# Interleaving the last norm of a transformer tower over three tiles on the Vector engine, and filling TensorE with constant products through a recurrence

## The chip, the cores and the metric

The kernel runs on one core of a Trainium2 chip. A core has TensorE (PE: matrix products; its weight loads are shown apart as PEld), the Vector engine (DVE), the Scalar engine (ACT), GpSimd (POOL) and SyncE (SP, which issues DMAs). The engines run side by side and wait for each other on semaphores; each takes its own instructions in their order in the program. The metric is the device time of one execution in microseconds (us); the median over the runs is quoted.

## The reference: what is computed

A small vision tower over 32 images of 3x64x64 pixels. Sixteen patches of an image and a class token make 17 tokens of 192 features, 544 tokens in all. Four parts follow, each with a layer norm in front and the input added back:

1. attention with mixing of the heads' scores before and after the softmax;
2. a mixture of 16 experts (top 4 of a softmax router);
3. a recurrence over the 17 tokens of every image;
4. a mixture of 8 experts (the best one for each token).

The change touches parts 3 and 4:

```
def step(h, ins):                      # part 3, for token t = 0..16
    bv, dc, ij = ins
    h_next = dc * quat_rotate(h, bv) + ij
    return (h_next, h_next)
_, hs = scan(step, h0, (biv_t, dec_t, inj_t))
y = (hs - mean(hs)) / sqrt(var(hs) + 1e-05) * gamma + beta
h = h + y
x = layernorm(h)                       # part 4
logits = x @ router_w                  # 8 experts; argmax picks one
out = combine over experts of relu(x @ Wi_e) @ Wo_e
h = h + out
```

So between the recurrence and the router there are two norms over the 192 features of each token: that of the states `hs` (norm 3 in the code) and that of the sum `h` (norm 4).

## The kernel before, in words

The 544 tokens lie in five tiles: four of 119 rows (seven images) and one of 68. Activations are kept both with a token in a partition (for norms) and turned, with a feature in a partition (for products). A product in single precision is made of rounded high and low parts, so a turned tile is taken out of PSUM twice: ACT writes the high part (`high_turned`, L428), DVE subtracts it from the original for the low part (`low_turned`, two instructions, L959 and L961).

All engines' programs are written out by hand, in the order in which the lines are called; nothing reorders them. Around the change they are as follows.

- **Walls.** PE multiplies the normed input by the weights of the recurrence (`wall`, through L1651) into PSUM banks 0 to 7. ACT and DVE take the results out and make, for every token, a 3x3 rotation with its decay, `rmat`. PE has nothing to do meanwhile.
- **Scan.** DVE alone computes the states, 16 steps in two chains of eight images: a product (L1430) and a sum (L1435) for each chain. From step 9 on PE runs `hold`: products of constants (L1927, 128x128 by 128x272) whose result nobody reads, 4 a step and 2 in the last, released by the step's product.
- **Norms.** PE turns the states back to a token in a partition (`states_turned(i)`, L2024, L2026, and L2028 with L2034 for tile 2, which lies over both halves of the partitions), one PSUM bank a tile. For each tile DVE then does, under `states_normed`, `summed` and `shifted`: statistics (bn_stats, L943), their mean and variance (bn_aggr, L944), `xw = (state - mean) * gamma` (L1444), reciprocal of the deviation (L1451), `h = xw * rstd + h` (L1454), bn_stats and bn_aggr again for norm 4, the reciprocal (L1461) and the shift `xn_off` (L1463). With the two of `low_turned` these are eleven. ACT supplies the square roots (`root(3, i)` and `root(4, i)`, L423), the normed rows `xn` (`scaled_shifted`, L749), their rounded copy (`high_rows`, L756) and `high_turned`. PE turns `xn` (`norm_turned(4, 4, i)`, L1636 and L1637) and, when both parts of a turned tile are there, multiplies it by the router's weights (`split_route(i)`, L1824 to L1828). Holds stand between these.
- **Routing and experts.** When the five products of the router are there, DVE finds each token's expert (from L1500), PE counts and sorts, and the eight blocks of the experts run on PE.

Inside DVE's program, `then(...)` makes the next instruction wait for the one just issued, and `mark(...)` only counts it.

## Time and profile before

| what | us |
|---|---|
| median of 3 runs | 401.79 |
| the three runs | 401.99, 400.30, 401.79 |
| the profiled execution, its own time | 400.97 |
| its span from first to last instruction | 399.2 |
| PE busy | 353.0 (88%) |
| DVE busy | 327.7 (82%) |
| ACT busy | 243.5 (61%) |
| POOL busy | 31.7 (8%) |

The span is 1.77 us shorter than the execution's own time, and the own time 0.82 us under the median. All rows below have their times from the start of the span. "Busy" of an engine counts the time in which an instruction of it runs; instructions of one engine can overlap at their ends, so a row's start to the next row's start says what an instruction costs its engine, and its duration when its result is there.

### The profile page before, as it was taken

The page shows a single profiled execution, that of the slowest core. Times are in us where ns is not written, and L with a number is a line of the kernel's source. Part 1 is how long each engine was busy: PE and PEld are TensorE (multiplying, and loading weights), DVE is VectorE, ACT ScalarE, POOL GpSimd, SP SyncE. Part 2 cuts the span into 40 slices and gives each one's busy share as a digit, 9 for nine tenths or more (in the row PEclk, how much of TensorE's full clock was granted, in tenths as well). Part 3 has the DMA queues.
Part 4 walks back from the last instruction along what each step waited for, and adds up shares of the span by engine and source line. Part 5 has one row for each costly group of instructions (what it writes and reads, how often), then busy time and mean ns, then how long its engine had stood idle before and what let it go on. Part 6 is the DMA issues. An engine that isn't in the chain of part 4 may idle for free.

```text
span 399.2 us, 8184 instructions
## 1 busy us (share of the span) xinstructions
PE 353.0 (88%) x2748; PEld 339.1 (85%) x2748; DVE 327.7 (82%) x782; ACT 243.5 (61%) x451; POOL 31.7 (8%) x61
## 2 busy tenths in 40 slices
PE   4999899989999999999999999770099899999991
PEld 4899768889999999999999999660088799999981
DVE  2798888798998888889898887789989888788741
ACT  1372667866776677677677766868006457777630
POOL 5020000200000000000000000210000051000004
PEclk9999999999999999999999999986586999999996
DMA  8902000394333331223333322020000055465101
GB/s 294 337 33 80 1 2 2 72 431 139 109 108 108 107 106 45 73 103 108 108 108 108 106 91 84 29 80 2 0 0 0 2 177 187 146 230 173 68 2 43
DMA packets 10701, 39.95 MB, mean 100 GB/s; under 512 B 1569, under 2 KB 2530, under 8 KB 10546
## 3 DMA queue, kind: packets, MB, share of 16 engines
q1 hardware_dynamic: 9154, 33.69, 25.5%
q0 software_dynamic: 1088, 5.48, 3.9%
q10 hardware_dynamic: 432, 0.43, 0.4%
q8 instruction: 15, 0.25, 0.2%
q14 instruction: 12, 0.10, 0.1%
HBM read 38.72 MB, written 0.87 MB: 99 GB/s over the span
## 4 chain that ended last, share of the span: by engine, by line
PE 75%; DVE 15%; ACT 5%; issue 2%; DMA 1%; POOL 1%; POOLq 0%; DVEq 0%
PE ps L1699 27%; PE ps L1651 14%; PE ps L1733 3%; PE ps L1873 3%; PE ps L1870 3%; PE ps L1874 3%; PE ps L1871 3%; PE ps L1868 3%; PE ps L1927 3%; PE ps L1665 2%; PE ps L2122 2%; PE ps L2123 2%; PE ps L2127 2%; PE ps L2124 2%; PE ps L2126 2%
## 5 line engine op out<-in xcount | busy, mean ns | idle before, releaser
L1699 PE MATMUL ps<-xs,w_hi 128*128 128x272 f32 x376 | 63.3, 290 | 1.9 <-ACT gact L580 0.8
L1699 PE MATMUL ps<-xs,w_lo 128*128 128x272 f32 x376 | 62.7, 288 | 0.0
L1699 PEld LDWEIGHTS ps<-xs,w_hi 128*128 128x128 f32 x376 | 53.1, 188 | 2.8 <-ACT gact L580 1.2
L1699 PEld LDWEIGHTS ps<-xs,w_lo 128*128 128x128 f32 x376 | 53.2, 188 | 0.0
L580 ACT ACTIVATE gact<-ps,b1x 128x544 f32<-128x544 f32 x48 | 34.3, 715 | 25.9 <-PE ps L1699 25.8
L587 ACT ACTIVATE lin<-ps,b1x 128x544 f32<-128x544 f32 x48 | 34.3, 714 | 23.1 <-PE ps L1699 23.1
L1927 PE MATMUL ps<-p_hl 128*128 128x272 f32 x104 | 21.2, 350 | 21.5 <-DVE rmat L1430 21.3
L1233 DVE TENSOR_TENSOR lin<-gact,lin 128x544 f32<-128x544 f32 x48 | 34.8, 725 | 5.0
L1699 PE MATMUL ps<-xa_lo,w_hi 128*128 128x272 f32 x188 | 38.8, 287 | 0.0
L1240 DVE TENSOR_TENSOR hid_lo<-lin,hid_hi 128x544 fp32r<-128x544 f32 x48 | 34.5, 718 | 2.5 <-ACT hid_hi L595 2.5
L1927 PEld LDWEIGHTS ps<-p_hl 128*128 128x128 f32 x104 | 17.2, 232 | 22.6 <-issue 21.8
L595 ACT ACTIVATE hid_hi<-lin 128x544 fp32r<-128x544 f32 x48 | 31.2, 650 | 4.8 <-DVE lin L1233 4.8
L1576 DVE SCALAR_TENSOR_TENSOR hid_lo<-ps,hid_hi 128x272 fp32r<-128x272 f32 x54 | 23.4, 437 | 12.8 <-ACT hid_hi L814 10.7
L1221 DVE SCALAR_TENSOR_TENSOR gact<-gact,comb_bc 128x544 f32<-128x544 f32 x45 | 32.4, 721 | 1.4 <-DMA comb_bc<-comb_dram 1.0
L814 ACT ACTIVATE hid_hi<-ps 128x272 fp32r<-128x272 f32 x54 | 21.4, 397 | 18.5 <-PE ps L1651 16.7
L1651 PE MATMUL ps<-xsrt,w_hi 128*128 (+1 forms) x162 | 29.3, 289 | 0.3 <-DVE hid_lo L1576 0.3
L1699 PEld LDWEIGHTS ps<-xa_lo,w_hi 128*128 128x128 f32 x188 | 29.4, 188 | 0.0
L1870 PE MATMUL ps<-hid_hi,w_hi 128*128 128x272 f32 x96 | 27.8, 289 | 0.7 <-DVE w_hi L1259 0.7
L1873 PE MATMUL ps<-hid_lo,w_hi 128*128 128x272 f32 x96 | 27.8, 290 | 0.5 <-ACT hid_hi L595 0.5
L1871 PE MATMUL ps<-hid_hi,w_hi 128*128 128x272 f32 x96 | 27.7, 289 | 0.0
L1874 PE MATMUL ps<-hid_lo,w_hi 128*128 128x272 f32 x96 | 27.7, 289 | 0.0
L1868 PE MATMUL ps<-hid_hi,w_hi 128*128 128x272 f32 x96 | 27.7, 288 | 0.0
(314 smaller groups left out, 882.4 us busy)
## 6 DMA issues: line engine op xcount, KB each, us to landing
raw<-in_w SPq DMA_DIRECT2D x25, 768.0 KB, 5.6
raw<-in_w SPq DMA_DIRECT2D x9, 576.0 KB, 3.9
raw<-in_w SPq DMA_DIRECT2D x16, 288.0 KB, 2.8
comb_bc<-comb_dram POOLq DMA_DIRECT2D x1, 3264.0 KB, 16.6
xp_sb<-in_xp SPq DMA_DIRECT2D x3, 357.0 KB, 6.2
pk_sb<-in_pk SPq DMA_DIRECT2D x1, 615.5 KB, 5.2
comb_bc<-comb_dram POOLq DMA_DIRECT2D x1, 544.0 KB, 9.4
hsrt<-rows_dram POOLq DMA_DIRECT2D x1, 388.0 KB, 3.6
```

The lines of the kernel that those rows point to most:

```text
L580: act.activation(gact[k][:, c, :].rearrange("p (a b) -> p a b", a=2), ps[:, bank:bank + 2, 0:HALF], ACT.Gelu_apprx_sigmoid, bias=b1x[:, ba ...
L587: act.activation(lin[b][:, c, :].rearrange("p (a b) -> p a b", a=2), ps[:, 6:8, 0:HALF], ACT.Identity, bias=b1x[:, bass.ds(6 * e + 3 + c, ...
L1233: dve.tensor_tensor(lin[b][:, c, :], gact[b][:, c, :], lin[b][:, c, :], ALU.mult).then_inc(s["aval"], 1)
L1240: dve.tensor_tensor(hid_lo[0][:, c, :], lin[b][:, c, :], hid_hi[0][:, c, :].bitcast(F32), ALU.subtract)\
L1651: ins = pe.matmul(dst, a, b, start=(n == 0), stop=(n == len(pairs) - 1), skip_group_check=True)
L1699: ins = pe.matmul(dsts[hh], w, x[:, hh * HALF:(hh + 1) * HALF], start=(n == 0), stop=(n == len(parts) - 1), skip_group_check=True)
L1868: pe.matmul(ps[:, ACC_BANKS[hh], 0:HALF], main, hi, start=False, stop=False, skip_group_check=True)
L1870: pe.matmul(ps[:, ACC_BANKS[hh], 0:HALF], low, hi, start=False, stop=False, skip_group_check=True)
L1871: pe.matmul(ps[:, ACC_BANKS[2 + hh], 0:HALF], tail, hi, start=False, stop=False, skip_group_check=True)
L1873: pe.matmul(ps[:, ACC_BANKS[hh], 0:HALF], main, lo, start=False, stop=end, skip_group_check=True)
L1874: pe.matmul(ps[:, ACC_BANKS[2 + hh], 0:HALF], tail, lo, start=False, stop=end, skip_group_check=True)\
L1927: pe.matmul(ps[:, bank, 0:HALF], p2_hi[:, 0:128], p2_hi[:, 0:HALF], start=True, stop=True, skip_group_check=True)
```

## The change

It has three parts.

1. **DVE and ACT.** The functions of the norms are cut into single instructions (`states_stats`, `states_mean`, `states_centred`, `states_scale`, `summed`, `summed_stats4`, `summed_mean4`, `scale4`, `shifted`). `then` becomes `mark`, and the wait on the earlier result stands in front of the instruction that reads it. The calls are written in an order in which those of three tiles alternate. ACT's calls are reordered to suit: three roots of norm 3 come first, and `high_rows` stands later.
2. **PE before and during the scan.** Holds start right behind the walls: 100 once `bvec_ready` is 3 (bank 0 has been read), then 5 in every step of the scan from the first on, 2 in the last. They write bank 0, not 7.
3. **PE in the norms.** The holds between its products become fewer: 9 to 4, 4 to 3, 8 to 4 and 3, 4 to 3. Behind `norm_turned(4, 4, 2)` the holds write bank 2, where the states of tile 2 were, so PE waits there until DVE has read them (`t_ready`).

The order of PE's instructions around the norms, before (`L2024` to `L2034` and `L2026` turn states, `L1636` and `L1637` turn `xn`, `L1927` are holds, `L1824` to `L1828` the router; `p_hl` is the array that holds the constants):

```order
L1927 MATMUL ps<-p_hl 128x272 x30
L2024 MATMUL ps<-ident,hs 119x64 x6
L2028 MATMUL ps<-ident,hs 119x64 x3
L2034 MATMUL ps<-ident,hs 119x64 x3
L1927 MATMUL ps<-p_hl 128x272 x8
L1636 MATMUL ps<-ident,xn 128x119
L1637 MATMUL ps<-ident,xn 64x119
L2026 MATMUL ps<-ident,hs 119x64 x3
L1927 MATMUL ps<-p_hl 128x272 x6
L1636 MATMUL ps<-ident,xn 128x119
L1637 MATMUL ps<-ident,xn 64x119
L2026 MATMUL ps<-ident,hs 68x64 x3
```

and now:

```order
L1995 MATMUL ps<-p_hl 128x272 x177
L2093 MATMUL ps<-ident,hs 119x64 x6
L2097 MATMUL ps<-ident,hs 119x64 x3
L2103 MATMUL ps<-ident,hs 119x64 x3
L1995 MATMUL ps<-p_hl 128x272 x8
L1704 MATMUL ps<-ident,xn 128x119
L1705 MATMUL ps<-ident,xn 64x119
L2095 MATMUL ps<-ident,hs 119x64 x3
L1995 MATMUL ps<-p_hl 128x272 x6
L1704 MATMUL ps<-ident,xn 128x119
L1705 MATMUL ps<-ident,xn 64x119
L2095 MATMUL ps<-ident,hs 68x64 x3
```

The 30 holds are 177, and the next turn of states (tile 3) is still behind the turn of the first `xn`; only the later holds are fewer.

DVE after the scan, before (`stats<-ps` are the statistics of norm 3, `stats<-h` those of norm 4):

```order
L943 BN_STATS stats<-ps 119x6
L944 BN_AGGR mv<-stats 119x2
L1444 SCALAR_TENSOR_TENSOR xw<-ps,mv,pk_sb 119x192
L1451 RECIPROCAL rstd<-sd 119x1
L1454 SCALAR_TENSOR_TENSOR h<-xw,rstd,h 119x192
L943 BN_STATS stats<-h 119x6
L944 BN_AGGR mv<-stats 119x2
L943 BN_STATS stats<-ps 119x6
L944 BN_AGGR mv<-stats 119x2
L1444 SCALAR_TENSOR_TENSOR xw<-ps,mv,pk_sb 119x192
```

and now:

```order
L1456 SCALAR_TENSOR_TENSOR xw<-ps,mv,pk_sb 119x192 x2
L1463 RECIPROCAL rstd<-sd 119x1 x2
L1472 SCALAR_TENSOR_TENSOR h<-xw,rstd,h 119x192
L1443 BN_STATS stats<-ps 119x6
L1479 BN_STATS stats<-h 119x6
L1450 BN_AGGR mv<-stats 119x2
L1486 BN_AGGR mv<-stats 119x2
L1472 SCALAR_TENSOR_TENSOR h<-xw,rstd,h 119x192
L1456 SCALAR_TENSOR_TENSOR xw<-ps,mv,pk_sb 119x192
L1479 BN_STATS stats<-h 119x6
L1492 RECIPROCAL rstd<-sd 119x1
```

The statistics of tile 1 stand in the second place, and those of tile 2 stand ahead of the statistics of norm 4 of tile 0.

At the end of the norms, now, from tile 4's `h` on (`68x192` rows are tile 4's):

```order
L1472 SCALAR_TENSOR_TENSOR h<-xw,rstd,h 68x192
L958 TENSOR_TENSOR xa_lo<-ps,xs 128x119
L960 TENSOR_TENSOR xs<-ps,xs 64x119
L1479 BN_STATS stats<-h 68x6
L958 TENSOR_TENSOR xa_lo<-ps,xs 128x119
L960 TENSOR_TENSOR xs<-ps,xs 64x119
L1486 BN_AGGR mv<-stats 68x2
L1492 RECIPROCAL rstd<-sd 68x1
L1500 SCALAR_TENSOR_TENSOR xn_off<-mv,rstd 68x1
L958 TENSOR_TENSOR xa_lo<-ps,xs 128x68
L960 TENSOR_TENSOR xs<-ps,xs 64x68
```

Before, the same stretch was:

```order
L1454 SCALAR_TENSOR_TENSOR h<-xw,rstd,h 68x192
L943 BN_STATS stats<-h 68x6
L944 BN_AGGR mv<-stats 68x2
L959 TENSOR_TENSOR xa_lo<-ps,xs 128x119
L961 TENSOR_TENSOR xs<-ps,xs 64x119
L1461 RECIPROCAL rstd<-sd 68x1
L1463 SCALAR_TENSOR_TENSOR xn_off<-mv,rstd 68x1
L959 TENSOR_TENSOR xa_lo<-ps,xs 128x119
L961 TENSOR_TENSOR xs<-ps,xs 64x119
L959 TENSOR_TENSOR xa_lo<-ps,xs 128x68
L961 TENSOR_TENSOR xs<-ps,xs 64x68
```

Now two pairs of `low_turned` (tiles 2 and 3) stand ahead of the last bn_aggr, and one (tile 2) ahead of the last bn_stats; before, one pair (tile 2) stood behind the last bn_aggr.

The diff:

```diff
--- before.py
+++ after.py
@@ -299,8 +299,8 @@
         CLEARED = 14
         GATE_BANK = 0
         HOLD_BANK = 4
-        STEP_BANK, LATE_BANK, ROUT_BANK = 7, 6, 5
-        HELD_FROM = 9
+        WALL_BANK, STEP_BANK, LATE_BANK, ROUT_BANK = 0, 7, 2, 5
+        HELD_TURN, HELD_STEP = 100, 5
         EMBED_FIRST = 3
         SPARE_BANK = 7
         WIDE = 6
@@ -756,31 +756,30 @@
                 act.activation(xcat[0:r, i, 0:DIM], xn[0:r, i, :], ACT.Copy).then_inc(cat_hi, 1)
 
             root(3, 0)
+            root(3, 1)
...
-
             exps(1, E1)
             act.wait_ge(count_mm, 1)
             act.activation(counts[:], ps[0:E1 * NTILES, COUNT_BANK, 0:128], ACT.Copy).then_inc(count_out, 1)
@@ -1435,54 +1434,123 @@
                     dve.tensor_reduce(state(t, chain), rmat[:, t, :, :, im].rearrange("p o c b -> p o b c"), AX_X, ALU.add)\
                        .then_inc(scan_step[chain], 1)
 
-            def states_normed(i):
+            counted = {}
+
+            def states_stats(i):
 
                 r = ROWS[i]
                 dve.wait_ge(ht_mm, i + 1)
-                row_stats(3, ps, i)
+                mark(dve.bn_stats(stats[0:r, i, :], ps[0:r, i, 0:DIM]))
+                counted["states", i] = own[0]
+
+            def states_mean(i):
+
+                r = ROWS[i]
+                dve.wait_ge(dve_step, counted["states", i])
+                dve.bn_aggr(mv[0:r, i, :], stats[0:r, i, :]).then_inc(ln[3]["mean"], 1)
+
+            def states_centred(i):
+
+                r = ROWS[i]
                 dve.wait_ge(ln[3]["mean"], i + 1)
                 dve.scalar_tensor_tensor(xw[0:r, i, :], ps[0:r, i, 0:DIM], mv[0:r, i, 0:1], p2("gamma", r), ALU.subtract,
                                          ALU.mult).then_inc(t_ready, 1)
 
+            def states_scale(i):
+
+                r = ROWS[i]
+                dve.wait_ge(ln[3]["sd"], i + 1)
+                mark(dve.reciprocal(rstd3[0:r, i:i + 1], sd[0:r, i:i + 1]))
+                counted["scale", i] = own[0]
+
             def summed(i):
 
                 r = ROWS[i]
-                dve.wait_ge(ln[3]["sd"], i + 1)
-                then(dve.reciprocal(rstd3[0:r, i:i + 1], sd[0:r, i:i + 1]))
+                dve.wait_ge(dve_step, counted["scale", i])
                 dve.wait_ge(base2_ready, i + 1)
                 dve.wait_ge(t_ready, NTILES + i + 1)
-                then(dve.scalar_tensor_tensor(h[0:r, i, 0:DIM], xw[0:r, i, :], rstd3[0:r, i:i + 1], h[0:r, i, 0:DIM], ALU.mult, ALU.add))
-                row_stats(4, h, i)
+                mark(dve.scalar_tensor_tensor(h[0:r, i, 0:DIM], xw[0:r, i, :], rstd3[0:r, i:i + 1], h[0:r, i, 0:DIM], ALU.mult, ALU.add))
+                counted["summed", i] = own[0]
+
+            def summed_stats4(i):
+
+                r = ROWS[i]
+                dve.wait_ge(dve_step, counted["summed", i])
+                mark(dve.bn_stats(stats[0:r, i, :], h[0:r, i, 0:DIM]))
+                counted["stats", i] = own[0]
+
+            def summed_mean4(i):
+
+                r = ROWS[i]
+                dve.wait_ge(dve_step, counted["stats", i])
+                dve.bn_aggr(mv[0:r, i, :], stats[0:r, i, :]).then_inc(ln[4]["mean"], 1)
+
+            def scale4(i):
+
+                r = ROWS[i]
+                dve.wait_ge(ln[4]["sd"], i + 1)
+                mark(dve.reciprocal(rstd[0:r, i:i + 1], sd[0:r, i:i + 1]))
+                counted["scale4", i] = own[0]
 
             def shifted(i):
 
                 r = ROWS[i]
-                dve.wait_ge(ln[4]["sd"], i + 1)
-                then(dve.reciprocal(rstd[0:r, i:i + 1], sd[0:r, i:i + 1]))
+                dve.wait_ge(dve_step, counted["scale4", i])
                 dve.wait_ge(ln[4]["mean"], i + 1)
                 dve.scalar_tensor_tensor(xn_off[0:r, i:i + 1], mv[0:r, i, 0:1], -1.0, rstd[0:r, i:i + 1], ALU.mult, ALU.mult)\
                    .then_inc(shift4, 1)
 
-            states_normed(0)
+            states_stats(0)
...
+
             def low_rows(i):
 
                 r = ROWS[i]
@@ -2005,10 +2073,11 @@
                 wall(n, 0)
                 wall(n, 1).then_inc(wall_mm, 1)
 
-            pe.wait_ge(inj_ready, 6)
-            for t in range(HELD_FROM, SEQ):
+            pe.wait_ge(bvec_ready, 3)
+            hold(HELD_TURN, WALL_BANK)
+            for t in range(1, SEQ):
                 pe.wait_ge(scan_step[1], 2 * t - 1)
-                hold(4 if t < SEQ - 1 else 2, STEP_BANK)
+                hold(HELD_STEP if t < SEQ - 1 else 2, WALL_BANK)
             for chain in range(2):
                 pe.wait_ge(scan_step[chain], 2 * SEQ - 2)
             pe.wait_ge(inj_ready, 6)
@@ -2044,7 +2113,7 @@
             hold(6, STEP_BANK)
             norm_turned(4, 4, 1)
             states_turned(4)
-            hold(9, STEP_BANK)
+            hold(4, STEP_BANK)
 
             def split_route(i):
 
@@ -2053,14 +2122,16 @@
                 route("rout", E1, ROUT_BANK, rt[1]["mm"], i)
 
             split_route(0)
-            hold(4, STEP_BANK)
+            hold(3, STEP_BANK)
             norm_turned(4, 4, 2)
+            pe.wait_ge(t_ready, NTILES + 3)
+            hold(4, LATE_BANK)
             split_route(1)
-            hold(8, LATE_BANK)
+            hold(3, LATE_BANK)
             norm_turned(4, 4, 3)
             hold(3, LATE_BANK)
             split_route(2)
-            hold(4, LATE_BANK)
+            hold(3, LATE_BANK)
             norm_turned(4, 4, 4)
             split_route(3)
             hold(3, LATE_BANK)
```

## Rows read from the trace of the kernel before

**Rows 1.** Windows: stretch, length, each engine's busy us (instructions), PE's granted clock, DMA.
```profile
160.00:200.00 40.00, 40.00 (x320) 40.00 (x320) 35.86 (x58) 28.06 (x43) 0.78 (x1) 1.00 0.29 96
267.60:288.80 21.20, 0.00 (x0) 0.00 (x0) 20.43 (x57) 10.76 (x15) 0.00 (x0) 0.61 0.00 1
295.20:299.60 4.40, 4.34 (x27) 4.13 (x26) 3.30 (x14) 1.11 (x4) 0.78 (x1) 0.99 0.00 0
299.60:306.20 6.60, 6.58 (x29) 5.26 (x28) 6.02 (x25) 4.50 (x13) 0.00 (x0) 0.50 0.00 0
```

**Rows 2.** Chain of waits: start us, us, engine, array written, line.
```profile
295.26 1.14 PE ps L2024 x6
...
298.62 1.33 PE ps L1927 x8
...
311.83 0.23 DVE gl L1500
```

**Rows 3.** Timeline of DVE, the norms: start us, us, line, operation; in brackets idle time before, and its releaser.
```profile
295.95 0.37 DVE L943 BATCH_NORM_STATS2 stats<-ps 119x6 f32<-119x192 f32 x1 [0.81 <-PE ps L2024]
...
297.98 0.18 DVE L944 BATCH_NORM_AGGREGATE mv<-stats 119x2 f32<-119x6 f32 x1
298.07 0.33 DVE L943 BATCH_NORM_STATS2 stats<-ps 119x6 f32<-119x192 f32 x1
298.44 0.18 DVE L944 BATCH_NORM_AGGREGATE mv<-stats 119x2 f32<-119x6 f32 x1
298.66 0.42 DVE L1444 SCALAR_TENSOR_TENSOR xw<-ps,mv,pk_sb 119x192 f32<-119x192 f32 x1
298.99 0.15 DVE L1461 RECIPROCAL rstd<-sd 119x1 f32<-119x1 f32 x1
299.18 0.16 DVE L1463 SCALAR_TENSOR_TENSOR xn_off<-mv,rstd 119x1 f32<-119x1 f32 x1
299.25 0.16 DVE L1451 RECIPROCAL rstd<-sd 119x1 f32<-119x1 f32 x1
...
300.40 0.33 DVE L943 BATCH_NORM_STATS2 stats<-ps 119x6 f32<-119x192 f32 x1
...
302.72 0.25 DVE L959 TENSOR_TENSOR xa_lo<-ps,xs 128x119 fp32r<-128x119 f32 x1
...
303.31 0.37 DVE L943 BATCH_NORM_STATS2 stats<-ps 119x6 f32<-119x192 f32 x1
...
308.09 0.36 DVE L943 BATCH_NORM_STATS2 stats<-h 68x6 f32<-68x192 f32 x1
308.48 0.18 DVE L944 BATCH_NORM_AGGREGATE mv<-stats 68x2 f32<-68x6 f32 x1
```

**Rows 4.** Timeline of PE, the norms.
```profile
299.98 0.46 PE L1636 MATMUL ps<-ident,xn 119*128 119x119 f32 x1
...
300.57 0.86 PE L2026 MATMUL ps<-ident,hs 64*119 64x64 f32 x3
...
308.57 0.27 PE L1636 MATMUL ps<-ident,xn 119*128 119x119 f32 x1
```

**Rows 5.** Timeline of ACT, the norms.
```profile
299.38 0.55 ACT L749 ACTIVATE xn<-h,xn_off,rstd 119x192 f32<-119x192 f32 x1 [0.42 <-DVE xn_off L1463]
...
308.98 0.37 ACT L428 ACTIVATE xs<-ps 128x238 fp32r<-128x238 f32 x1
```

**Rows 6.** Timeline of DVE, scan: start us, us, line, operation, count.
```profile
281.60 0.48 DVE L1430 TENSOR_TENSOR rmat<-rmat,hs 128x72 f32<-128x72 f32 x2
...
288.24 0.45 DVE L1430 TENSOR_TENSOR rmat<-rmat,hs 128x72 f32<-128x72 f32 x2
...
294.19 0.50 DVE L1430 TENSOR_TENSOR rmat<-rmat,hs 128x72 f32<-128x72 f32 x2
```

**Rows 7.** Timeline of DVE around the end of the walls.
```profile
265.36 0.44 DVE L1365 SCALAR_TENSOR_TENSOR cross<-bvec 128x272 f32<-128x272 f32 x1
...
268.22 0.44 DVE L1384 SCALAR_TENSOR_TENSOR half_ang<-turns,h_norm 128x272 f32<-128x272 f32 x1
```

More of the change, by code:

```diff
@@ L777, in _ @@
             high_rows(3)
+            high_turned(4, 3)
             root(4, 4)
-            high_turned(4, 3)
             scaled_shifted(4)
@@ L1464, in shifted @@
                    .then_inc(shift4, 1)
-            states_normed(0)
-            summed(0)
-            states_normed(1)
-            shifted(0)
-            summed(1)
-            states_normed(2)
+            states_stats(0)
+            states_stats(1)
+            states_mean(0)
+            states_mean(1)
+            states_centred(0)
+            states_centred(1)
+            states_scale(0)
+            states_scale(1)
+            summed(0)
+            states_stats(2)
+            summed_stats4(0)
+            states_mean(2)
+            summed_mean4(0)
+            summed(1)
+            states_centred(2)
+            summed_stats4(1)
+            scale4(0)
+            states_scale(2)
+            shifted(0)
+            summed_mean4(1)
+            summed(2)
+            states_stats(3)
+            scale4(1)
+            summed_stats4(2)
             shifted(1)
-            summed(2)
+            states_mean(3)
+            summed_mean4(2)
+            states_centred(3)
             low_turned(4, 0)
-            states_normed(3)
+            scale4(2)
+            states_scale(3)
             shifted(2)
             summed(3)
+            states_stats(4)
+            summed_stats4(3)
+            states_mean(4)
+            summed_mean4(3)
+            states_centred(4)
             low_turned(4, 1)
-            states_normed(4)
+            scale4(3)
+            states_scale(4)
             shifted(3)
@@ L1482, in _ @@
             low_turned(4, 2)
+            summed_stats4(4)
+            low_turned(4, 3)
+            summed_mean4(4)
+            scale4(4)
             shifted(4)
-            low_turned(4, 3)
             low_turned(4, 4)
```

13 lines of the change are left out of this document (6 added, 7 removed).

## The prediction

> **What bounds the kernel now.** I read the windows first, then the chain of waits, then the timelines of DVE, PE and ACT between the scan and the router. The windows [rows 1] show PE full in the experts, then, from the end of the walls to 288.8 PE does nothing, DVE is busy for 20.4 of 21.2 us, and the granted clock of PE falls from 1.0 to 0.5 on the way (mean 0.61). Behind the scan's 30 holds it is back (0.99 from 295.2 to 299.6), and then 0.50 to 306.2. So the turns of states of tiles 0 to 2 already run at the high clock, 2.4 GHz, in this execution, and what follows at the low one, 1.2 GHz.
>
> The chain [rows 2] puts nearly all of 295.3 to 311.8 on PE. That is misleading: holds end on time, and an instruction that follows others on its engine is put down to the engine. The timeline of DVE says what sets the end [rows 3]: its only idle time there before the last `low_turned` is 0.81 us ahead of the first statistics, and each instruction starts within 0.05 us of what it needs on DVE itself. The statistics of tile 2 start at 300.40, though PE had its states at 298.62 [rows 2]. DVE's own chain is the bound, and it costs 300.40 - 298.07 = 2.33 us a tile before the two `low_turned`.
>
> **What the weave can take away.** An instruction that reads the one before it waits for its end; an unrelated one starts earlier. From [rows 3], as start to next start: bn_aggr 0.22 before its reader, 0.09 otherwise; `xw` 0.33 before a reciprocal that doesn't need it, before a reader 0.42, its duration, and some 0.03, and so does `h`, the same kind and size; the shift 0.07; the reciprocal 0.19 before its reader, an estimated 0.08 otherwise. bn_stats never stands before an unrelated instruction: the ends are its 0.37 before a reader and a guess of 0.24; I take 0.30, its 0.37 less about the overlap of `xw` (0.42 to 0.33). Nine instructions of a tile then cost 0.30 + 0.10 + 0.33 + 0.08 + 0.33 + 0.30 + 0.10 + 0.08 + 0.07 = 1.69, and 5 tiles save 5 x 0.64 = 3.2 us, if nothing else comes late. Something does.
>
> The Trainium skill (VectorE: DVE Perf Modes, The DRAIN you can't avoid) says that one cannot skip the wait for an empty pipeline by leaving out semaphores, so that weaving would save nothing; it adds that an instruction that is not held starts earlier. The rows bear out the addition (0.33 us after a start of 0.42 us). By the rule alone the saving of 3.2 us would be 0.
>
> **What is late next: the states of tiles 2 and 3.** I put the new order on the rows' times, all at PE's high clock.
>
> - Statistics of tile 0 at 295.95, of tile 1 about 0.5 later (six turns for two tiles take 1.14, rows 2). Two bn_aggr, two `xw`, two reciprocals and the first `h` follow. DVE would be at the statistics of tile 2 at 298.1; PE has the states at 298.6 [rows 2]. They start at 298.7, 1.7 us ahead of before, and all behind them has waited 0.6 us: the statistics of norm 4 of tile 0 are queued there.
> - From 298.7 come bn_stats twice, bn_aggr twice, `h`, `xw`, bn_stats: 0.30 + 0.30 + 0.10 + 0.10 + 0.33 + 0.33 + 0.30 = 1.76, so the reciprocal of norm 4 of tile 0 at 300.46 and its shift at 300.67. ACT starts `xn` 0.20 later, as from 299.18 to 299.38, and PE turns it 0.60 after that, as from 299.38 to 299.98 [rows 3 to 5]: 301.5. Before it did so at 299.98. The turn of tile 3's states is queued on PE behind this. Two turns of `xn` take an estimated 0.14 (half of one's 0.27 at the high clock, since they overlap [rows 4]) and three of states 0.57 (half of the 1.14), with 0.1 until DVE sees them: 302.3. DVE has run out of work at 301.2 and idles 1.1 us. Statistics of tile 3: 302.3, before 303.31.
> - From there to the last bn_stats DVE goes without a break: four bn_stats at 0.30, four bn_aggr 0.44 (two of them wait 0.02 for their statistics), two `xw` and two `h` 1.32, five reciprocals and three shifts 0.71, three pairs of `low_turned` at 0.59 (302.72 to 303.31) 1.77: 5.44. The last bn_stats starts at 307.7, before at 308.09. Three pairs stand in this stretch where before there was one, which is why the lead of 1.0 is down to 0.4.
> - Ahead of the last bn_aggr now stands the pair of tile 3. By the same count its shift is at 306.8; PE turns it at 307.6, ACT takes it out 0.41 later, as from 308.57 to 308.98, and needs 0.37 [rows 4, 5], so the pair starts at 308.4 and ends at 309.0. The last bn_aggr starts there, before at 308.48: 0.5 behind.
> - The tail from it to the router's first sum was 311.83 - 308.48 = 3.35. The pair of tile 2 no longer stands between it and the reciprocal: some 0.2 less. The sum starts at 309.0 + 3.15 = 312.1 or 312.2. The weave costs **+0.3 us**. With bn_stats at 0.26 or 0.34 instead of 0.30 this is 0 or +0.6.
>
> **The holds.** After the walls 100 of them run. In the experts 320 products of the same 272 columns take 40 us, 0.125 each [rows 1], so they last 12.5 of the 14 us until the first step [rows 6], and nothing is queued behind them but other holds. They take no reader's bank. What hides them is that PE had nothing to do. In the open is only what they cost DVE. The scan shows it [rows 6]: from 281.60 to 288.24 eight steps take 6.64 us, 0.83 each, with PE idle; from 288.24 to 294.19 seven take 5.95, 0.85 each, with holds. Eight more steps with holds: 8 x 0.02 = **+0.2 us**. Five holds at the high clock are about 0.65 us, under a step; the two of the last step end before the last sum. Before the scan, operations of 272 columns on DVE take 0.44 beside the walls and 0.44 without PE [rows 7], so I put that stretch at 0; the scan's 3% over its 13.4 us would be 0.4, the upper end, and a gain has no reason there.
>
> The clock at the end of the scan becomes certain instead of lucky. In this execution it rose in time, so the term is 0 in the sum; where it doesn't, the turns of tiles 0 to 2 cost up to half their 3.3 us more, of which DVE, which needed tile 2 only 1.7 us later, paid little.
>
> **The clock in the norms.** It fell at 299.6, after turns of states and eight holds, and was 0.5 for 6.6 us [rows 1]. That cost nothing, since DVE never waited for PE. Now PE's turns of tile 3 are in DVE's way, the work before them is the same, PE idles for 1.9 us more ahead of them, and 11 of the 37 later holds are gone. At the low clock the turns of `xn` took 0.59 (299.98 to 300.57) and not 0.14, those of tile 3 0.86 and not 0.57 [rows 4]: +0.7 for tile 3's statistics if the spell covers these alone, +1.2 if it lasts 6.6 us, since the turns of tiles 3 and 4 at the end are then late as well, and 0 if it doesn't come. I take **+0.6**, between none and the longer one and nearest to the short one. It is no more than a choice: the same execution shows both levels in this stretch.
>
> **The sum.** +0.3 + 0.2 + 0.6 = +1.1 on the profiled execution's 400.97: 402.1. Its time is 0.8 under the median of the runs shown and 0.7 over the fastest, and the three runs spread over 1.7. I don't carry the 0.8 over: a part of what makes the other runs longer can be a clock that rose later than here, and that the early holds take away. 402.1 it is, 0.3 over the median.
>
> **Rivals.**
>
> - *The weave pays (faster).* For it: the 1.69 a tile is made of few pairs; if the 26 instructions after 302.3 cost 0.05 less each, DVE gains 1.2. A further 0.8 would come in runs whose clock rose late, and 0.5 if the last pair finds its turn ready. 401.79 - 2.4 = 399.4. Against it: the two waits on PE don't depend on any of this, and 1.1 us before 302.3 is idle anyway. Chance 0.20.
> - *No wait, no price.* The clock stays high through the norms, and the scan's 0.2 is all: 401.0 to 401.5. For it: PE comes warm out of 100 and 77 holds. Against it: it came warm out of 30 at 295.2 and fell all the same. Chance 0.22.
> - *The low clock outlasts the norms (slower).* With fewer holds and longer waits PE is emptier from 299.6 to 311.8 than before. If the clock falls before tile 3 is turned and isn't back by 309.9, the turns of the last `xn` and the router's products are low too: the last sum at about 315, 3.2 later; every further microsecond of low clock in the sort and the experts, where PE bounds, costs 0.5. 404.3 and up. [...] Chance 0.13.
> - *Unrelated instructions don't overlap in the new pairs.* bn_stats 0.40, `h` 0.45 and reciprocal 0.20 everywhere: the same path ends at 313.7, +1.9; with the scan 403.1, with the clock 403.7. By the Trainium skill's rule (VectorE: DVE Perf Modes, The DRAIN you can't avoid) it would be so. Against it: `xw` and bn_aggr do overlap. Chance 0.05.
>
> My forecast, that the weave gives its gain back to the waits for PE, has 0.40, with a range of its own from 401.2 to 403.2.
>
> About 0.5%, 2.0 us, is what a measurement of this kernel can tell from no change. Faster than 399.8: most of the first rival, 0.17. Slower than 403.8: the third, a part of the fourth and the tail of the forecast, 0.20. Between: 0.63. The range of 8 in 10 goes from 399.4, the first rival's time, to 404.0, short of the third's.
>
> **What would show it.** In the profile after: statistics of tile 2 with idle time before them, released by PE's turn, and those of tile 3 with some 1.1 us, at about 302.3 or later; the last bn_aggr behind a pair of `low_turned` that waited for ACT; eight early steps of the scan at 0.85; holds from the end of the walls with the clock at 1.0 through the scan, and a low spell between 297 and 306. The prediction is wrong if the statistics of tile 3 start without idle time, if bn_stats before an unrelated instruction costs 0.24 or less, or if the clock stays up all through the norms and the time still moves by more than a microsecond.

## The result: 1.2% slower

| | median us | runs | ratio to the kernel before, with 95% interval |
|---|---|---|---|
| before | 401.89 | 4 | |
| changed | 407.65 | 4 | 1.0126 [1.0088, 1.0163] |
| changed, measured again | 406.24 | 6 | 1.0110 [1.0077, 1.0144] |

The forecast was 402.1, in a range from 399.4 to 404.0. The median 407.65 includes one slow run of 424.4 us at a mean granted clock of 0.825, which the ratio leaves out; the three others are 405.36, 407.18 and 408.13, so their median is 407.18. The profiled execution took 407.18 us against 400.97: 6.2 us to be found.

The same stages in both traces, each from the start of one named instruction to the start of the next:

| stage | before | changed | difference |
|---|---|---|---|
| to DVE's first `bvec` after the walls | 263.69 | 264.65 | +0.96 |
| to the first copy of the scan (L1421 / L1420) | 17.64 | 17.86 | +0.22 |
| scan, to the statistics of tile 0 | 14.62 | 14.89 | +0.27 |
| norms, to the router's first sum | 15.88 | 18.28 | +2.40 |
| routing, to the first `pick` | 3.25 | 3.83 | +0.58 |
| sort, to the first product of the experts | 4.36 | 6.10 | +1.74 |
| the rest | 79.7 | 79.7 | 0.0 |

### The profile page after: what moved, and what is told of

Its sections match the earlier page's. It is cut to its first block, busy times and chain, and to the rows that moved or that the text cites. A ratio compares the mean times of both kernels' runs of the same rounds, so it can differ in the third digit from the quotient of the medians.

```text
span 405.3 us, 8461 instructions
## 1 busy us (share of the span) xinstructions
PE 377.1 (93%) x2887; PEld 361.6 (89%) x2887; DVE 327.4 (81%) x782; ACT 243.3 (60%) x451; POOL 31.5 (8%) x61
## 4 chain that ended last, share of the span: by engine, by line
PE 78%; DVE 11%; ACT 6%; issue 2%; DMA 1%; POOL 1%; POOLq 0%; DVEq 0%
PE ps L1767 27%; PE ps L1719 14%; PE ps L1995 5%; PE ps L1801 3%; PE ps L1941 3%; PE ps L1938 3%; PE ps L1942 3%; PE ps L1939 3%; PE ps L1936 3%; PE ps L1733 2%; PE ps L2193 2%; PE ps L2194 2%; PE ps L2195 2%; PE ps L2198 2%; PE ps L2197 2%
## 5 line engine op out<-in xcount | busy, mean ns | idle before, releaser
L1995 PE MATMUL ps<-p_hl 128*128 128x272 f32 x243 | 42.3, 326 | 2.4 <-DVE rmat L1429 2.4
L1995 PEld LDWEIGHTS ps<-p_hl 128*128 128x128 f32 x243 | 36.6, 215 | 4.7 <-DVE rmat L1429 4.3
```

Of the source, the lines that this page charges most:

```text
L1995: pe.matmul(ps[:, bank, 0:HALF], p2_hi[:, 0:128], p2_hi[:, 0:HALF], start=True, stop=True, skip_group_check=True)
```

## The profile after

The windows first: stretch, length, busy us (instructions) of PE, weight loads, DVE, ACT, POOL, then PE's granted clock and two DMA figures. They are the stretches of [rows 1] from the walls on, and the routing and the sort behind them.

```profile
268.20:282.80 14.60, 12.73 (x102) 12.51 (x100) 13.68 (x24) 11.42 (x16) 0.00 (x0) 1.00 0.01 2
283.30:296.60 13.30, 13.28 (x77) 11.50 (x77) 13.29 (x62) 0.00 (x0) 0.00 (x0) 0.88 0.00 0
296.70:300.10 3.40, 3.34 (x20) 3.14 (x19) 2.11 (x9) 0.48 (x2) 0.78 (x1) 0.99 0.02 5
300.10:310.20 10.10, 9.50 (x40) 8.09 (x41) 7.34 (x37) 5.04 (x17) 0.00 (x0) 0.50 0.00 0
310.20:315.70 5.50, 3.76 (x31) 3.35 (x31) 2.77 (x13) 3.54 (x8) 0.00 (x0) 0.99 0.00 1
315.70:319.50 3.80, 3.04 (x16) 2.41 (x16) 2.67 (x15) 1.91 (x5) 0.00 (x0) 0.68 0.00 0
319.50:325.60 6.10, 6.10 (x33) 5.93 (x33) 5.15 (x20) 0.69 (x2) 0.00 (x0) 0.64 0.00 0
```

And the two last stretches in the kernel before:

```profile
311.80:315.10 3.30, 2.53 (x17) 1.94 (x17) 2.72 (x16) 1.95 (x5) 0.00 (x0) 1.00 0.00 0
315.10:319.40 4.30, 3.92 (x31) 3.84 (x31) 4.30 (x18) 0.70 (x3) 0.00 (x0) 1.00 0.00 0
```

The holds do what was expected of them up to 283.3: 12.7 us, clock 1.0. The clock still dips once in the scan (0.88) and is up for the turns of states, as before. Then it falls at about the same place as before, 300.1 or 3.4 us behind the first turn of states (4.3 before), and here stays low for 10.1 us, where [rows 1] has 6.6. It comes back for 5.5 us and falls again, so that the last part of the routing and most of the sort run at the low level; before, both were at 1.0.

The chain of waits (start, us, what), where [rows 2] had PE's turns of tiles 0 and 1, the holds behind tile 2, and the router's sum:

```profile
296.71 1.14 PE ps L2093 x6
...
303.44 0.78 PE ps L2095 x3
...
315.68 0.22 DVE gl L1568
...
318.94 1.20 PE ps L1995 x4
320.14 5.63 PE ps L2160 x30
```

PE's turn of tile 3 is on the chain, and the 30 products of the sort take 5.63 us. Four holds stand right ahead of them for 1.20 us; no run takes these four out.

DVE from the scan to the router (start, us, line, operation; idle time before it in brackets), against [rows 3, 6]:

```profile
282.79 0.48 DVE L1429 TENSOR_TENSOR rmat<-rmat,hs 128x72 f32<-128x72 f32 x2
...
289.62 0.48 DVE L1429 TENSOR_TENSOR rmat<-rmat,hs 128x72 f32<-128x72 f32 x2
...
295.65 0.48 DVE L1429 TENSOR_TENSOR rmat<-rmat,hs 128x72 f32<-128x72 f32 x2
...
297.40 0.85 DVE L1443 BATCH_NORM_STATS2 stats<-ps 119x6 f32<-119x192 f32 x2 [0.81 <-PE ps L2093]
...
300.11 0.36 DVE L1443 BATCH_NORM_STATS2 stats<-ps 119x6 f32<-119x192 f32 x1 [0.48 <-PE ps L2103]
300.39 0.34 DVE L1479 BATCH_NORM_STATS2 stats<-h 119x6 f32<-119x192 f32 x1
300.65 0.16 DVE L1450 BATCH_NORM_AGGREGATE mv<-stats 119x2 f32<-119x6 f32 x1
300.77 0.18 DVE L1486 BATCH_NORM_AGGREGATE mv<-stats 119x2 f32<-119x6 f32 x1
...
301.21 0.41 DVE L1456 SCALAR_TENSOR_TENSOR xw<-ps,mv,pk_sb 119x192 f32<-119x192 f32 x1
301.54 0.35 DVE L1479 BATCH_NORM_STATS2 stats<-h 119x6 f32<-119x192 f32 x1
301.81 0.15 DVE L1492 RECIPROCAL rstd<-sd 119x1 f32<-119x1 f32 x1
301.87 0.14 DVE L1463 RECIPROCAL rstd<-sd 119x1 f32<-119x1 f32 x1
301.99 0.16 DVE L1500 SCALAR_TENSOR_TENSOR xn_off<-mv,rstd 119x1 f32<-119x1 f32 x1
...
304.26 0.36 DVE L1443 BATCH_NORM_STATS2 stats<-ps 119x6 f32<-119x192 f32 x1 [1.72 <-PE ps L2095]
...
310.10 0.28 DVE L958 TENSOR_TENSOR xa_lo<-ps,xs 128x119 fp32r<-128x119 f32 x1 [0.89 <-ACT xs L428]
...
310.72 0.36 DVE L1479 BATCH_NORM_STATS2 stats<-h 68x6 f32<-68x192 f32 x1
311.86 0.28 DVE L958 TENSOR_TENSOR xa_lo<-ps,xs 128x119 fp32r<-128x119 f32 x1 [0.77 <-ACT xs L428]
...
312.47 0.18 DVE L1486 BATCH_NORM_AGGREGATE mv<-stats 68x2 f32<-68x6 f32 x1
...
315.68 0.22 DVE L1568 TENSOR_REDUCE gl<-ps 119x32 f32<-119x64 f32 x1
```

The reader is to see three things. Where nothing has to be waited for, the weave works: the two bn_stats start 0.28 apart (300.11, 300.39), two bn_aggr 0.12, `xw` to bn_stats 0.33 (301.21, 301.54), a reciprocal to the next 0.06 (301.81, 301.87). The statistics of tiles 2 and 3 wait for PE, 0.48 and 1.72 us. And near the end two pairs of `low_turned` wait for ACT, 0.89 and 0.77 us, with the last statistics of norm 4 behind the first and the last bn_aggr behind the second.

PE, against [rows 4], and ACT, against [rows 5]:

```profile
302.78 0.46 PE L1704 MATMUL ps<-ident,xn 119*128 119x119 f32 x1 [0.60 <-ACT xn L749]
...
303.37 0.85 PE L2095 MATMUL ps<-ident,hs 64*119 64x64 f32 x3
304.15 1.73 PE L1995 MATMUL ps<-p_hl 128*128 128x272 f32 x6
...
308.23 1.03 PE L1995 MATMUL ps<-p_hl 128*128 128x272 f32 x3
309.06 0.40 PE L1704 MATMUL ps<-ident,xn 119*128 119x119 f32 x1
```

```profile
302.18 0.55 ACT L749 ACTIVATE xn<-h,xn_off,rstd 119x192 f32<-119x192 f32 x1 [0.85 <-DVE xn_off L1500]
...
307.93 0.35 ACT L756 ACTIVATE xcat<-xn 119x192 fp32r<-119x192 f32 x1
309.70 0.37 ACT L428 ACTIVATE xs<-ps 128x238 fp32r<-128x238 f32 x1 [1.42 <-PE ps L1705]
```

The wait at 310.10 is PE's: ACT rounded tile 2's `xn` at 307.93, so `xn` was there, but PE had holds and the router's products of tile 0 in its queue, three of the holds at 308.23 for 1.03 us, and turned it only at 309.06. At the high clock, where 100 take 12.7 us, three take 0.4.

## The experiments

Each kernel ran beside the kernel before on the same chip. "Norms", "routing" and "sort" are the stages of the table above, read from each kernel's profile; "low" is the time in a stage at the low clock, counted from windows of 1 us. The holds in front of and between the turns and products of the norms were miscounted ahead of the result: there are 45 before the change and 37 after it, 8 fewer and not 11, and bare takes out 37 and not the 31 that its expectation names; the 6 behind the last product of the router are in neither number.

| kernel | median us | ratio, 95% interval | norms (low) | routing | sort (low) |
|---|---|---|---|---|---|
| before | 401.9 to 402.2 | | 15.88 (6.8) | 3.25 | 4.36 (0) |
| changed | 407.65 | 1.0126 [1.0088, 1.0163] | 18.28 (10.2) | 3.83 | 6.10 (4.4) |
| changed again | 406.24 | 1.0110 [1.0077, 1.0144] | 19.60 (16.4) | 3.84 | 5.76 (3.7) |
| weave_only | 407.74 | 1.0139 [1.0113, 1.0165] | 19.49 (10.2) | 3.84 | 5.88 (3.9) |
| early_only | 403.50 | 1.0039 [1.0017, 1.0060] | 15.89 (6.8) | 3.24 | 5.89 (3.4) |
| fewer_only | 402.51 | 1.0010 [0.9990, 1.0031] | 16.10 (10.2) | 3.25 | 5.87 (3.4) |
| weave_early | 408.07 | 1.0140 [1.0112, 1.0167] | 20.70 (15.2) | 3.83 | 6.33 (4.9) |
| bare | 404.57 | 1.0066 [1.0044, 1.0088] | 17.30 (14.1) | 3.84 | 5.25 (2.5) |
| turns_first_bare | 403.75 | 1.0048 [1.0023, 1.0074] | 15.80 (13.1) | 3.83 | 5.71 (3.6) |
| turns_first_pairs_later | 402.51 | 1.0028 [1.0002, 1.0054] | 14.73 (11.8) | 3.83 | 6.31 (4.9) |
| dense | 405.70 | 1.0099 [1.0066, 1.0133] | 20.60 (10.2) | 3.25 | 4.37 (0) |
| before_bare | 403.13 | 1.0035 [1.0016, 1.0054] | 16.19 (13.3) | 3.84 | 5.65 (3.4) |
| woven_best | 402.38 | 1.0016 [0.9999, 1.0033] | 14.73 (11.9) | 3.84 | 6.27 (4.7) |
| woven_gaps | 401.65 | 0.9999 [0.9976, 1.0021] | 14.73 (11.7) | 3.84 | 4.85 (1.6) |
| woven_count | 401.84 | 1.0011 [0.9986, 1.0036] | 14.75 (11.3) | 3.03 | 5.35 (2.7) |
| gaps_count | 402.21 | 0.9991 [0.9972, 1.0010] | 14.72 (11.7) | 3.04 | 6.68 (5.7) |
| gaps_full | 401.56 | 0.9982 [0.9962, 1.0001] | 14.91 (12.8) | 3.03 | 6.22 (4.7) |
| gaps_packed | 402.26 | 1.0017 [0.9995, 1.0038] | 16.13 (6.8) | 2.95 | 5.88 (3.4) |

The last three columns are of one execution each, the medians are of 4 to 12 runs. The walls, which no run changes, end anywhere from 263.3 to 265.2 us in these profiles, so a difference of a microsecond between two profiled executions proves nothing by itself; the stages are what is compared.

**One part at a time.** weave_only takes the new order of DVE and ACT alone, all holds as before the change (the diff is against the changed kernel):

```
-            pe.wait_ge(bvec_ready, 3)
-            hold(HELD_TURN, WALL_BANK)
-            for t in range(1, SEQ):
+            pe.wait_ge(inj_ready, 6)
+            for t in range(HELD_FROM, SEQ):
...
-            hold(4, STEP_BANK)
+            hold(9, STEP_BANK)
...
-            hold(3, LATE_BANK)
+            hold(8, LATE_BANK)
```

> The kernel before with the new order on DVE and ACT alone; holds as before. Theory A (PE's low clock in the norms and in the sort costs the time, because PE has less work there and DVE now waits for PE's turns): statistics of tile 3 start with over 1 us idle, released by PE; with the 11 later holds kept the clock is back at 1.0 before the sort; 401.9 + 1.0 to 1.8 = 403 to 403.7. Rival B (the early holds cost it): no change, 401.5 to 402.5. Rival C (the weave alone costs it all): 406 to 408.

The whole loss is here: +5.6 us on the medians. Its stages and two of DVE's waits:

```profile
297.50:317.00 19.50, 16.59 (x92) 14.55 (x93) 12.20 (x57) 9.03 (x26) 0.11 (x1) 0.74 0.00 1
317.00:320.90 3.90, 3.13 (x16) 2.50 (x17) 2.75 (x16) 1.95 (x5) 0.00 (x0) 0.63 0.00 0
320.90:326.70 5.80, 5.80 (x33) 5.63 (x33) 4.95 (x20) 0.69 (x2) 0.00 (x0) 0.66 0.00 0
```

```profile
304.40 0.36 DVE L1444 BATCH_NORM_STATS2 stats<-ps 119x6 f32<-119x192 f32 x1 [1.72 <-PE ps L2095]
...
311.60 0.28 DVE L959 TENSOR_TENSOR xa_lo<-ps,xs 128x119 fp32r<-128x119 f32 x1 [2.26 <-ACT xs L429]
...
313.20 0.28 DVE L959 TENSOR_TENSOR xa_lo<-ps,xs 128x119 fp32r<-128x119 f32 x1 [0.62 <-ACT xs L429]
```

19.5 us of norms, 1.2 more than in the changed kernel with a low spell as long: PE's queue holds 9 and 8 holds where that has 4 and 3, and the pair of tile 2 waits 2.26 us for them (ACT's copy comes behind PE's turn). Rival C had the total right. Theory A had the waits for PE and a quarter of the size, and its clock of 1.0 before the sort did not come.

early_only has only the early holds:

```
-            pe.wait_ge(inj_ready, 6)
-            for t in range(HELD_FROM, SEQ):
+            pe.wait_ge(bvec_ready, 3)
+            hold(HELD_TURN, WALL_BANK)
+            for t in range(1, SEQ):
```

> The kernel before with the 100 holds behind the walls and 5 in each step of the scan, nothing else. Theory A: DVE's order hides a low clock, so only the scan's own price: +0.2 to +0.5, 402.0 to 402.5. Rival B (177 holds make the clock fall later or lower, or slow DVE): +3 or more, 405 and up, with a low clock in the sort. Rival C: no change.

It costs 0.4% [0.2, 0.6], and 403.50 is 1 us above what was expected. In the profile 0.29 us of that is in the scan (14.91 against 14.62) and 0.17 ahead of it. All eight profiles with early holds have 14.87 to 14.92 for the scan, and nine of the ten without have 14.59 to 14.63 (gaps_full has 14.98). Ahead of the scan DVE's operations of 272 columns still take 0.44, as in [rows 7]; what got longer there are the writes of `rmat`, 1.64 and 3.00 us where they took 1.54 and 2.93. The rest is a low spell of 3.4 us in the sort; whether the early holds bring it isn't shown, since fewer_only, without them, has the same one. On top of the weave they cost nothing that the runs separate (weave_early against weave_only, both 1.014).

fewer_only has only the later holds of the changed kernel:

```
-            hold(9, STEP_BANK)
+            hold(4, STEP_BANK)
...
-            hold(8, LATE_BANK)
+            hold(3, LATE_BANK)
```

> The kernel before with only the later holds cut from 37 to 26 and moved to bank 2. Theory A: the norms are bound by DVE as before and take the same time, but the clock comes back later, and if it is low in the sort that costs up to 1.7 us: 402 to 404. Rivals B and C: no change, 401.5 to 402.3.

No change that can be told, though its low spell in the norms is as long as the changed kernel's, 10.2 us: the norms take 16.10. A low clock alone does little to the old order.

weave_early is the changed kernel with its later holds as before:

```
-            hold(4, STEP_BANK)
+            hold(9, STEP_BANK)
...
-            hold(3, LATE_BANK)
+            hold(8, LATE_BANK)
```

> The changed kernel with the later holds as before (9, 4, 8, 3, 4, 3), so that only the first two parts of the change are left. Theory A: the low spell ends before the sort, whose 30 products take 4.0 us and not 5.8: 2 us less than the changed kernel, 405.0 to 405.8. Rival B: as the changed kernel, 407 to 408. Rival C: as the kernel with the weave alone.

The theory failed in this, and rival C had it: more holds did not end the low spell before the sort. The norms take 20.70 us, 2.4 and 1.1 more than in the two profiles of the changed kernel, and the total is that of weave_only.

**Taking out what stands in the way.** bare has no hold left in the norms:

```
-            hold(8, STEP_BANK)
             norm_turned(4, 4, 0)
             states_turned(3)
-            hold(6, STEP_BANK)
             norm_turned(4, 4, 1)
...
```

> The changed kernel without any hold between the turns and the router's products in the norms (31 holds out); the holds behind the router, in the scan and after the walls stay. Theory E (the weave puts PE's turns in DVE's way, and at the low clock the holds queued ahead of them cost double): from the first statistics to the router's sum 17.5 to 18.0 us where the changed kernel takes 18.3, at the low clock throughout; the sort low as well; total 406.5 to 407.5. Rival F (the holds are what keeps the clock up, and only that matters): the norms as long or longer, sort and first experts low, 408 to 410. Rival G (the order on DVE alone costs it): no change.

404.57, 2.6 us less than the 407.18 of the first measurement of the changed kernel and 1.7 less than the 406.24 of the second, and 2 us under the 406.5 that theory E expected at least: the holds cost more than it had put. The norms ran at a lower mean clock than in the first profile:

```profile
297.80:315.10 17.30, 9.73 (x48) 7.65 (x47) 12.11 (x57) 9.15 (x26) 0.13 (x1) 0.59 0.00 0
```

```profile
304.71 0.36 DVE L1443 BATCH_NORM_STATS2 stats<-ps 119x6 f32<-119x192 f32 x1 [1.72 <-PE ps L2095]
...
311.02 0.28 DVE L958 TENSOR_TENSOR xa_lo<-ps,xs 128x119 fp32r<-128x119 f32 x1 [0.48 <-ACT xs L428]
```

PE is busy for 9.7 of 17.3 us and the norms are 1.0 and 2.3 us shorter than in the two profiles of the changed kernel. The waits say where: the statistics of tile 3 wait 1.72 us as before, but the pairs of tiles 2 and 3, which waited 0.89 and 0.77 us there (0.90 and 1.63 in after_again), now wait 0 and 0.48. So the holds cost mainly through the pairs, and the wait of tile 3 has another cause. That rules out rival F, by which taking out holds only lowers the clock and so costs time, and G, by which nothing changes. The kernel is still 0.66% slower than the one before.

turns_first_bare moves the turns of tiles 3 and 4 ahead of the first `xn`:

```
             states_turned(2)
+            states_turned(3)
+            states_turned(4)
             norm_turned(4, 4, 0)
-            states_turned(3)
             norm_turned(4, 4, 1)
-            states_turned(4)
```

> As bare, and the turns of states of tiles 3 and 4 stand ahead of the turn of the first xn. Theory E: statistics of tile 3 no longer wait, norms 15.3 us at the high clock and 15.8 to 16.2 at the low one, against 15.9 in the kernel before; what is left over the kernel before is the sort at the low clock, 1.7 us, and the scan: 403.5 to 404.5. Rival F: as bare, 407 or more. Rival G: as bare.

```profile
297.30:313.10 15.80, 9.26 (x47) 7.61 (x48) 12.04 (x57) 9.05 (x26) 0.10 (x1) 0.59 0.01 2
```

turns_first_pairs_later moves, besides, the pairs of `low_turned` at the end:

```
             summed(4)
-            low_turned(4, 2)
             summed_stats4(4)
-            low_turned(4, 3)
+            low_turned(4, 2)
             summed_mean4(4)
             scale4(4)
             shifted(4)
+            low_turned(4, 3)
             low_turned(4, 4)
```

with ACT's `root(4, 4)` ahead of `high_turned(4, 3)`.

> As turns_first_bare, and in the last tile the statistics of norm 4 and their bn_aggr stand ahead of the low_turned pairs of tiles 2 and 3, ACT's last root ahead of its copy of tile 3. Theory E: the norms take 14.5 to 15.2 us, 0.7 to 1.4 less than in the kernel before; with the sort at the low clock 402.5 to 403.5, at the high one 401 to 402. Rivals F and G: over 406.

```profile
297.80:312.60 14.80, 9.56 (x48) 7.63 (x48) 11.95 (x58) 8.98 (x26) 0.14 (x1) 0.60 0.01 2
```

15.80 and 14.73 us of norms, inside or at the edge of what was expected, at a clock of 0.59 and 0.60: the turns ahead give 1.5 us, the pairs later 1.1. So the weave does save DVE time, 1.15 us against the kernel before, once neither PE's queue nor a pair is in its way. DVE's busy time says the same, 11.95 us here and 13.65 in before_bare below. (The old order with the turns and pairs moved was not run.) What keeps the total at 402.5 is behind the norms: routing and sort at the low clock, 2.5 us more than before in this profile.

**More holds, and fewer.** dense:

```
-            states_turned(1)
+            hold(2, STEP_BANK)
+            states_turned(1)
+            hold(2, STEP_BANK)
             states_turned(2)
-            hold(8, STEP_BANK)
+            hold(14, STEP_BANK)
...                            # 8, 6, 6, 6, 5, 4, 10, 4 and 10 further on
```

> The changed kernel with more holds: 2 behind each of the first two turns of states, then 14, 8, 6, 6, 6, 5, 4, 10, 4, 4 and 10 where it has 8, 6, 4, 3, 4, 3, 3, 3, 3, 3 and 6. Rival F: the clock stays at 1.0 through the norms and the sort; norms 16.5 to 17.5 us, sort 4.0, total 403 to 404.5. Theory E, if the clock falls all the same: every hold counts double ahead of a turn, norms 22 us and more, total 410 or more; if it stays up, as F.

```profile
297.20:307.50 10.30, 10.24 (x46) 9.14 (x46) 5.99 (x29) 2.97 (x11) 0.14 (x1) 0.62 0.01 2
307.50:317.80 10.30, 9.68 (x71) 8.75 (x71) 6.20 (x29) 6.01 (x17) 0.00 (x0) 0.88 0.00 1
317.80:325.40 7.60, 6.96 (x52) 6.30 (x52) 7.02 (x34) 2.69 (x7) 0.00 (x0) 1.00 0.01 2
```

The clock fell all the same, with PE busy for 10.2 of 10.3 us; the norms take 20.6, and rival F, which had the clock at 1.0 throughout, is refuted again. Theory E's 22 us and 410 were too high. From 317.8 on it is 1.0, and routing and sort take 3.25 and 4.37 as in the kernel before. This is the one woven kernel of which both halves can be read: what the holds cost in the norms, and what the high clock gives behind them, 2.3 us against the changed kernel.

before_bare takes the 45 holds out of the kernel before:

```
-            hold(8, STEP_BANK)
             norm_turned(4, 4, 0)
             states_turned(3)
-            hold(6, STEP_BANK)
...
```

> The kernel before, its old order on DVE and ACT, without the 45 holds between the turns and the router's products in the norms. Theory E: DVE alone bounds the old norms, so they stay at 15.9 us at any clock; the clock stays low through the routing and the sort, which costs 0.6 and 1.5 to 1.9: 403.5 to 404.5, about where the woven order without holds stands (404.6). If the holds cost the old order something too, it gets faster.

```profile
295.70:311.90 16.20, 10.21 (x48) 7.73 (x47) 13.65 (x57) 9.93 (x26) 0.13 (x1) 0.59 0.00 1
311.90:315.80 3.90, 3.84 (x16) 3.10 (x17) 2.73 (x16) 1.82 (x5) 0.00 (x0) 0.50 0.01 4
315.80:321.40 5.60, 5.60 (x33) 5.43 (x33) 4.99 (x20) 0.69 (x2) 0.00 (x0) 0.70 0.00 0
```

+1.1 us on the medians. In the profile the norms grow by 0.3 and routing and sort by 1.9, with the clock at 0.50 and 0.70 there. In the old order the 45 holds in PE's queue are no cost, since behind the first statistics DVE waits for no turn until the last pair, and they are a small gain. In the woven order it is the other way: 407.74 with them (weave_only), 404.57 without any (bare, which also pays for the early holds).

woven_best is turns_first_pairs_later without the early holds:

> turns_first_pairs_later without the holds behind the walls and in the scan's first eight steps (from step 9 on 4 a step, as before the change). Theory E: 0.46 us less, 0.17 between walls and scan and 0.29 in the scan: 402.0. If the early holds are worth something in the norms, it gets slower than 402.5.

Against turns_first_pairs_later the lines of early_only's diff are taken back. 14.62 in the scan, 0.30 less; total 402.38 against 402.51, which the runs don't separate; 402.0 was expected.

woven_gaps puts 15 holds where PE waits anyway:

```
             states_turned(4)
+            hold(6, STEP_BANK)
             norm_turned(4, 4, 0)
+            hold(3, STEP_BANK)
             norm_turned(4, 4, 1)
...                            # then 1, 2, 2 and 1
```

> woven_best with 15 holds back, 6, 3, 1, 2, 2 and 1, each where PE waits for xn or for low_turned even at the low clock, so that none stands in a needed turn's way for more than 0.3 us. Theory E: norms 14.7 to 15.2 us; if the added work brings the clock back before the sort, routing 3.25 and sort 4.4 us: 400.0 to 400.5, faster than the kernel before by 1.5; if not, 402.

The norms stay at 14.73: these holds are free. In the profile the clock is back early in the sort, which takes 4.85 us, but not before it, and the total is that of the kernel before: the expected 1.5 us did not come.

woven_count leaves out the four holds between the two counting products:

```
             pe.matmul(ps[0:128, PLACE_BANK, 0:slots], later[0:TILE, :], flat, ...)
-            hold(4, LATE_BANK)
             pe.wait_ge(count_out, 1)
```

> woven_best without the four holds between the two products that count the tokens of each expert. At the low clock they take 1.2 us and the second product is ready 0.6 earlier: routing 3.25 us instead of 3.83, total 401.4, unless the clock comes back later in the sort for it.

Routing 3.03 instead of 3.84: these four cost 0.8 us at the low clock, since the second product is queued behind them. The totals (1.0011 against 1.0016) don't separate the two kernels.

**After these, what was still open.** after_again is the changed kernel unaltered:

> The changed kernel, unaltered, in more runs beside the kernel before. Its first four gave 405.4, 407.2, 408.1 and 424.4. If the order is the cause, 407 to 408, with the norms at 18 to 21 us; if a part was the walls' low spell, which moves from run to run in both, 405.5 to 406.5.

```profile
296.10:315.70 19.60, 17.86 (x84) 15.89 (x85) 12.21 (x57) 9.33 (x26) 0.12 (x1) 0.58 0.00 1
```

406.24, a little under the 407 expected, with a longer low spell and 19.6 us of norms, and with the walls ending at 263.50 where the kernel before has 263.69, so that the 0.96 us there in the first profile were chance. The two measurements together say 1.1 to 1.3%.

gaps_count, gaps_full and gaps_packed have no counting holds and 15, 24 and 34 holds in the norms, `hold(6)` and `hold(3)` above being 8 and 4, and 10 and 5, and in gaps_packed one more hold ahead of and behind the turn of tile 2:

> woven_gaps without the four holds between the counting products. Theory E: norms 14.7, routing 3.0 to 3.25 instead of 3.84, sort 4.4 to 4.9: 0.6 less than woven_gaps (401.65), 401.0.

> gaps_count with 24 holds in the norms where it has 15: 8, 4, 2, 3, 1, 1, 3 and 2. If fuller PE brings the clock back inside the norms, routing 3.0 to 3.25 and sort 4.4 while the norms stay under 15.2: 400.5 to 401.0. If it doesn't, each hold ahead of a turn costs 0.25: norms 15.5 and more, 401.5 to 402.5.

> As gaps_full with 34 holds: 1 and 1 around the turn of tile 2, then 10, 5, 3, 4, 2, 2, 4 and 2. PE is full from the first turn on. Clock back after about 7 us of the low spell, as in the kernel before; the holds in the way cost 0.5 to 1.5 in the norms (15.3 to 16.2): 401.0 to 402.0. If the clock stays low for 10 us as in the kernel dense, 403 or more.

```profile
296.10:311.00 14.90, 14.84 (x71) 13.51 (x71) 12.00 (x57) 8.95 (x26) 0.00 (x0) 0.57 0.00 1
```

In gaps_full PE is busy for 14.84 of 14.9 us and the clock is 0.57: filling PE's time did not bring it back. In gaps_packed it came back after 6.8 us, but its norms are 1.2 us longer than those of gaps_full and its total is no lower. gaps_count and gaps_packed missed what was expected of them by 1.2 and 0.3 us; gaps_full's norms, 14.91, are shorter than the 15.5 expected for a clock that stays low. gaps_full is the lowest median of all, 401.56, 0.18% under the kernel before, with an interval that just reaches 1.0001. A version clearly faster than the kernel before was not found.

## Why the prediction was wrong

The steps, in its order:

- **The weave and what is late next: right, to a tenth or two.** From the statistics of tile 0 it put those of tile 2 at +2.75 (measured 300.11 - 297.40 = 2.71), the shift of tile 0 at +4.72 (4.59), the turn of its `xn` at +5.55 (5.38), the statistics of tile 3 at +6.35 at the high clock or 0.7 more at the low one (6.86), the tail from the last bn_aggr at 3.15 (3.21). bn_stats before an unrelated instruction, taken at 0.30, costs 0.28. The rival that the new pairs don't overlap is refuted. turns_first_bare and turns_first_pairs_later confirm that tile 3's turn and the two pairs eat the gain: 1.5 and 1.1 us.
- **The early holds: small and right in kind.** +0.29 in the scan (forecast 0.2; its first eight steps take 0.85 each in the changed kernel, 282.79 to 289.62, as it said) and +0.17 ahead of it, which it put at 0; early_only as a whole costs 0.4%, with a low spell in the sort.
- **"The clock in the norms ... I take +0.6": this is the step that failed.** Two things in it were wrong. The spell was taken as one that covers the turns of tile 3 alone or lasts 6.6 us; it lasted 10.2 us in the first profile, and in the second it covered 16.4 of the norms' 19.6. And the price was put on the turns alone, where it falls on every hold queued ahead of a needed turn. The sum had no wait for tile 2's pair and 0.4 us for tile 3's; they waited 0.89 and 0.77 us in the first profile, 2.26 and 0.62 in weave_only. From the statistics of tile 3 to the last bn_aggr it put 6.7 us; it took 8.2. The norms cost +2.4 and +3.7 instead of the +0.9 of the sum (0.3 for the weave, 0.6 for the clock). Removing the holds gave back 1.0 and 2.3 of it in spite of the low clock, so that much is shown to be the queue. The 1.4 us that bare's norms still have over the kernel before went away with the order of the turns and pairs; what they would be at the high clock no run shows. The clock by itself is worth 0.2 to 0.3 in the old order (fewer_only, before_bare).
- **Routing and sort: not in the sum.** They were written into the third rival only, at 0.13, and cost +0.58 and +1.4 to +1.7. At the low clock the sort's 30 products take 5.63 us on the chain, and four holds stand ahead of the count. dense, with the clock at 1.0 there, has 3.25 and 4.37 as before.
- **The rival that came nearest** is that one. Its condition was a fall before tile 3 is turned, which came, and no return by 309.9 on the scale of the kernel before, 13.95 us behind the first statistics. In the first profile the clock was back after 12.8 us (310.2 - 297.40), a microsecond sooner, and then fell again; in the second it was not back. So the condition held in one of two, while its price for the norms, +3.2, lies between the two profiles and its total, 404.3 and up, covers both. It deserved more than 0.13: the kernel before showed 6.6 us of low clock behind turns of states, and the change kept those turns and put PE's work behind them on the path.
- **Slips that change nothing.** 8 of the later holds are gone and not 11 of 37, an argument for the longer spell and no term of the sum. In the first rival 26 x 0.05 is 1.3 and not 1.2, and the 2.4 that it takes off is not the sum of the gains it names (1.2, 0.8 and 0.5).

What stays open: why the spell takes 6.8 us of the norms in some profiles and 10 to 16 in others. It doesn't follow the number of holds (6.8 with 45 and with 34, 10.2 with 45, 37 and more, 12.8 with 24), and the changed kernel itself had 10.2 and 16.4. And with one profile a kernel, how often the kernel before has a low sort isn't shown; its runs of up to 403.7, and in two comparisons 405, suggest that it sometimes does.

## What to carry to other kernels

Constant products that keep an engine warm are free only while nobody waits for what is queued behind them. An interleaving that takes the slack from the other engine turns them into latency, at the low clock at twice the price (six took 1.73 us in the norms, where 100 had taken 12.7), so move the needed work ahead of them first, and size them for the low clock. When a trace shows a clock spell that costs nothing, read what it would cost once its cover is gone, over its whole length and over the stages behind it, before giving it a small number.
